# Two attentions over 2048 tokens: a third PSUM bank for the maxima, the causal mask as a matrix product, and the softmax shift as rows of the operands

## What is computed

```python
x = L0_attn_x;  xn = layernorm(x)
# first attention: 16 heads of 8, causal
q, k, v = xn @ Wq.T, xn @ Wk.T * 8**-0.5, xn @ Wv.T
attn = softmax(where(causal, q k^T, -inf))
s = layernorm(attn v) * gamma + beta, then @ Wo.T
# the FFN block: 16 query heads, 4 shared key/value heads, then experts
h = rmsnorm(xn);  q, k, v = h @ Wq + bq, h @ Wk + bk, h @ Wv + bv
q, k = rmsnorm(rope(q)) * qn_w, rmsnorm(rope(k)) * kn_w
out = softmax(where(causal, q k^T / sqrt(8), -inf)) v, gated by sigmoid(out @ Wg + bg)
x1 = xn + out @ Wo + bo
y = the top expert of 8 for each token of rmsnorm(x1)
result = x + s * silu(x1 + y)
```

## Time and profile before

| | us |
|---|---|
| median of 3 runs | 800.93 (800.92 to 801.12) |
| the profiled execution | 802.43 |
| its span, first to last instruction | 800.7 |
| PE (matmuls) busy | 673.8 (84%) |
| VectorE busy | 548.2 (68%) |
| ScalarE busy | 600.1 (75%) |
| GpSimd busy | 184.6 (23%) |
| mean granted clock of TensorE | 0.977 of full |

### The profile page before, as it was taken

The page is one execution under the profiler, slowest core; times in us unless marked ns, Lnnn a source line. Parts: engine busy times, 40 slices in busy tenths (PEclk is TensorE's granted clock), DMA queues, the critical chain, the costliest instruction groups (busy, mean ns, idle before and its releaser), DMA issues.

```text
span 800.7 us, 28924 instructions
## 1 busy us (share of the span) xinstructions
PE 673.8 (84%) x12295; PEld 218.3 (27%) x12295; DVE 548.2 (68%) x1492; ACT 600.1 (75%) x682; POOL 184.6 (23%) x357
## 2 busy tenths in 40 slices
PE   1368877889989899899988888888888988999994
PEld 1122222222222222222222222223232222355542
DVE  6885431777778777676678877777787877545436
ACT  1167977778877788888987787877777687888882
POOL 4363104011012011201120103120032055225241
PEclk9997989999999999999999999999999999999996
DMA  3112224104112000100021001100000050435523
GB/s 117 56 50 61 59 73 150 52 3 78 47 38 63 23 3 6 49 22 2 3 64 33 3 2 48 49 3 2 3 3 2 2 167 27 122 100 172 159 79 89
DMA packets 35852, 41.72 MB, mean 52 GB/s; under 512 B 5916, under 2 KB 26396, under 8 KB 35724
## 3 DMA queue, kind: packets, MB, share of 16 engines
q1 hardware_dynamic: 34052, 36.69, 15.6%
q0 software_dynamic: 1248, 2.57, 1.0%
q10 hardware_dynamic: 424, 0.62, 0.2%
HBM read 29.39 MB, written 10.24 MB: 49 GB/s over the span
## 4 chain that ended last, share of the span: by engine, by line
PE 55%; DVE 19%; ACT 8%; issue 8%; SPq 7%; DMA 2%; POOL 0%; POOLq 0%; ACTq 0%; DVEq 0%
PE PS L1030 25%; PE PS L979 13%; PE PS L1008 8%; ACT PR L908 7%; DVE MP L1349 7%; PE PS L934 6%; DVE PS L1346 4%; SPq L529 2%; SPq L530 2%; PE PS L1040 1%; DMA k_shared<-WORKQ 1%; SPq L532 1%; SPq L533 1%; DVE MP L1346 1%; DVE OT L1370 1%
## 5 line engine op out<-in xcount | busy, mean ns | idle before, releaser
L908 ACT ACTIVATE PR<-PS,QKM 128x1024 f32<-128x1024 f32 (+1 forms) x288 | 287.8, 1068 | 40.3 <-PE PS L1008 39.3
L908 ACT ACTIVATE PR<-PS 128x1024 f32<-128x1024 f32 (+1 forms) x288 | 264.9, 976 | 61.6 <-PE PS L1008 59.5
L1349 DVE TENSOR_REDUCE MP<-PS 128x1 f32<-128x512 f32 x384 | 248.6, 685 | 75.9 <-PE PS L979 73.6
L1030 PE MATMUL PS<-PR,VA 128*18 128x512 f32 (+3 forms) x2560 | 295.0, 543 | 1.2 <-DVE OT L1370 0.6
L1008 PE MATMUL PS<-QA,KA 56*32 56x512 bf16 (+7 forms) x5120 | 237.6, 355 | 31.4 <-ACT PR L908 26.8
L979 PE MATMUL PS<-KA,QA 56*32 56x512 f16 (+3 forms) x2560 | 203.9, 350 | 45.6 <-DVE MP L1349 26.5
L720 POOL TENSOR_SCALAR_AFFINE_SELECT PR<-PR 128x256 f32<-128x256 f32 x256 | 102.3, 417 | 454.7 <-ACT PR L908 452.1
L1346 DVE CUSTOM_DVE_ANT_0 PS<-PS,CON 128x128 f32<-128x128 f32 (+3 forms) x256 | 122.9, 506 | 49.7 <-PE PS L979 46.2
L979 PEld LDWEIGHTS PS<-KA,QA 56*32 56x32 bf16 x2560 | 58.2, 89 | 212.6 <-DVE MP L1349 116.4
L1008 PEld LDWEIGHTS PS<-QA,KA 56*32 56x32 f16 (+1 forms) x5120 | 67.3, 90 | 161.5 <-ACT PR L908 138.5
L1030 PEld LDWEIGHTS PS<-PR,VA 128*18 128x18 f32 x2560 | 46.8, 97 | 94.1 <-issue 87.4
(11 more groups left out here) (178 smaller groups left out, 390.3 us busy)
## 6 DMA issues: line engine op xcount, KB each, us to landing
WORKQ<-in_W SPq DMA_DIRECT2D x16, 450.0 KB, 3.9
QA<-q_parts SPq DMA_DIRECT2D x124, 48.0 KB
WORKK<-in_W SPq DMA_DIRECT2D x7, 450.0 KB, 3.3
KA<-k_parts SPq DMA_DIRECT2D x64, 48.0 KB
q_parts<-WORKQ SPq DMA_DIRECT2D x4, 384.0 KB, 2.9
q_parts<-WORKK SPq DMA_DIRECT2D x4, 384.0 KB, 3.9
expert_tokens<-ZERO SPq DMA_DIRECT2D x1, 1483.5 KB, 10.2
KA<-k_shared SPq DMA_DIRECT2D x60, 24.0 KB
```

The costliest lines, as they stand in the source:

```text
L908: act.activation(PR[:, (2 * n + p) % RING, :, 0:w], PS[:, 2 * p:2 * p + 2, 0:w], ACT.Exp, bias=shift)\
L1030: last = pe.matmul(PS[STRIP * hh:STRIP * hh + 2 * VW, 6, q0:CH], VA[:, slot % 2, kb, hh, VW * (1 - place):VW * (3 - place)], PR[:, (2 * n ...
L1349: dve.reduce_max(top, bank, AX).then_inc(s_mr, 1)
```

## The change

1. `bank_uses` gives each unit the bank of 4, 5 and 7 that was used the longest time ago, by whatever work.
2. Diagonal units get their mask on PE: four more matmuls of 32 rows and 128 columns add a table of 0 and -1e30 to the last 128 columns. The table and a 32 x 32 identity are bf16, loaded by one DMA, and cast by GpSimd at step 22. VectorE uses the plain maximum for all units, and the table of constants is shorter by what the mask took.
3. The FFN's constant shift is written into rows 56 and 57 of `QA` as two bf16 numbers, by four DMAs a buffer: buffers 0 and 1 at the start, buffer 2 when slot 5 is loaded. The FFN's scores use 58 rows, and the exponentials have no bias tile. In buffer 0 the rows still hold the constant when slot 3 comes.
4. The six DMAs of ones go to the start of SP's queue, with eight of the shift behind them.

The diff, cut to its core:

```diff
@@ bank_uses
+    def oldest():
+        return min((4, 5, 7), key=lambda bank: max(i for i, use in enumerate(out) if use[1] == bank))
...
         for u in (*parts[0], *parts[1]):
-            out.append((("unit", unit_number(u)), 4 + unit_number(u) % 2, "M"))
+            out.append((("unit", unit_number(u)), oldest(), "M"))
...
         for u in parts[2]:
-            out.append((("unit", unit_number(u)), 4 + unit_number(u) % 2, "M"))
+            out.append((("unit", unit_number(u)), oldest(), "M"))
@@ sync
             sp.dma_start(LAT[:, :], late).then_inc(s_lc, 16)
+            sp.dma_start(EXTRA[:, 0:NMASK], masks).then_inc(s_ml, 16)
...
+            def constant_shift(b):
+                for row in (STACK, STACK + 1, 64 + STACK, 64 + STACK + 1):
+                    sp.dma_start(QA[row:row + 1, b, :, :, :].rearrange("p c h (t s) -> p (c h t) s", s=P),
+                                 SHB[:, row % 2, :].unsqueeze(1).broadcast_to([1, NC * PAIRS * BPC, P])).then_inc(s_cs, 16)
+
+            sp.wait_ge(s_1b, 1)
+            for b in range(NBUF):
+                ones(b)
+            sp.wait_ge(s_cb2, 1)
+            constant_shift(0)
+            constant_shift(1)
...
-            sp.wait_ge(s_1b, 1)
-            for b in range(NBUF):
-                ones(b)
             for c in range(NC):
                 store_first(c, 0)
...
                         load(sp, k, c, (0, 1))
+                    if k == FFN_SLOT:
+                        constant_shift(k % NBUF)
@@ gpsimd
+                if n == 22:
+                    gp.wait_ge(s_ml, 16)
+                    gp.tensor_copy(MASK[:, :], EXTRA[:, 0:NMASK]).then_inc(s_cm, 1)
@@ scalar
-                        shift = QKM[:, 0:1] if SLOT_GROUP[SEQ[n][0]] < NKV else 0.0
-                        act.activation(PR[:, (2 * n + p) % RING, :, 0:w], PS[:, 2 * p:2 * p + 2, 0:w], ACT.Exp, bias=shift)\
+                        act.activation(PR[:, (2 * n + p) % RING, :, 0:w], PS[:, 2 * p:2 * p + 2, 0:w], ACT.Exp)\
@@ tensor, max_unit
-                bank = PS[:, 4 + u % 2, :]
+                bank = PS[:, BANK["unit", u], :]
...
                     last = pe.matmul(bank[r:r + STRIP, 0:w], QA[rows, b, c, pr, q:q + STRIP],
-                                     KA[rows, b, kc, pr, 0:w], start=True, stop=True)
+                                     KA[rows, b, kc, pr, 0:w], start=True, stop=kc < c)
+                if kc == c:
+                    pe.wait_ge(s_cm, 1)
+                    for r in range(0, P, STRIP):
+                        last = pe.matmul(bank[r:r + STRIP, w - P:w], MASK[64 * e:64 * e + 64, M_EYE:M_EYE + STRIP],
+                                         MASK[64 * e:64 * e + 64, r // STRIP * P:(r // STRIP + 1) * P], start=False, stop=True)
@@ tensor, scores
-                    rows = slice(64 * e, 64 * e + (STACK if ffn else ROWS))
+                    rows = slice(64 * e, 64 * e + ROWS)
@@ vector
+            link(dve.tensor_copy(SHB[:, 0, :], QKM[0:1, 0:1].broadcast_to([1, P])))
+            dve.tensor_tensor(SHB[:, 1, :], QKM[0:1, 0:1].broadcast_to([1, P]), SHB[:, 0, :], ALU.subtract)\
+               .then_inc(s_cb2, 1)
@@ vector, max_unit
-                bank = PS[:, 4 + u % 2, 0:w]
-                if kc == qb // BPC:
-
-                    dve.tensor_tensor_reduce(out=bank, in0=bank, in1=CON[:, K_CM + CH - w:K_CM + CH], scale=1.0, scalar=NEG,
-                                             op0=ALU.add, op1=ALU.max, accum_out=top).then_inc(s_mr, 1)
-                else:
-                    dve.reduce_max(top, bank, AX).then_inc(s_mr, 1)
+                dve.reduce_max(top, PS[:, BANK["unit", u], 0:w], AX).then_inc(s_mr, 1)
```

More of the change, by code:

```diff
@@ L291, with build @@
 NL = 912
-K_ID, K_TRI, K_CM, K_EARLIER, K_BEFORE, K_RANK, K_TOK, K_SPARE, K_TILE, K_J = 0, 128, 256, 768, 904, 968, 976, 992, 1015, 1038
-NK = 1054
-def build(nc, x, front, late, const, W12, out):
+K_ID, K_TRI, K_EARLIER, K_BEFORE, K_RANK, K_TOK, K_SPARE, K_TILE, K_J = 0, 128, 256, 392, 456, 464, 480, 503, 526
+NK = 542
+M_EYE = BPC * P
+NMASK = M_EYE + STRIP
+def build(nc, x, front, late, const, masks, W12, out):
     with ExitStack() as ctx:
@@ L324, in build @@
         ZERO = sb("ZERO", [P, ROW])
+        MASK = sb("MASK", [P, NMASK], BF16)
         ONEB = sb("ONEB", [2, P], F16)
@@ L332, in build @@
         HS = sb("HS", [P, 3, BPC * 20])
+        SHB = sb("SHB", [1, 2, P], BF16)
         SC = sb("SC", [P, 5])
@@ L447, in build @@
         s_one = sem("shift_ones_placed")
+        s_cb2 = sem("constant_shift_built")
+        s_cs = sem("constant_shift_placed")
+        s_ml = sem("masks_loaded")
+        s_cm = sem("masks_cast")
         s_sq2 = sem("key_weights_squared")
@@ L998, in scores @@
                     loaded(slot, c)
-                    if not ffn:
-                        pe.wait_ge(s_one, 32 * NBUF)
+                    pe.wait_ge(s_one, 32 * NBUF)
+                    if ffn:
+                        pe.wait_ge(s_cs, 64 * (2 if slot < FFN_SLOT else 3))
+                    else:
                         before = sum(1 for j in range(slot) if j % NBUF == b and SLOT_GROUP[j] >= NKV)
@@ L1658, in pack_const @@
     a[:, K_TRI:K_TRI + P] = p[None, :] > p[:, None]
-    a[:, K_CM + CH - P:K_CM + CH] = np.where(p[None, :] > p[:, None], NEG, 0.0)
     for t in range(1, T + 1):
@@ L1670, in pack_const, with pack_masks @@
     return a
+def pack_masks():
+    a = np.zeros((2, 64, NMASK), np.float32)
+    i = np.arange(STRIP)
+    for r in range(BPC):
+        a[:, :STRIP, r * P:(r + 1) * P] = np.where(np.arange(P)[None, :] > r * STRIP + i[:, None], NEG, 0.0)
+    a[:, :STRIP, M_EYE:] = np.eye(STRIP)
+    return a.reshape(P, NMASK)
 def kernel(**inputs):
@@ L1679 @@
     named = [("x", i["L0_attn_x"]), ("front", pack_front(i)), ("late", pack_late(i)), ("const", pack_const()),
+             ("masks", pack_masks()),
              ("W12", np.concatenate([i["L0_ffn_W1"],
```

## The result

| | before | changed |
|---|---|---|
| median, us | 800.92 (799.74 to 801.12, 4 runs) | **764.49** (762.16 to 765.30, 4 runs) |
| ratio to before | 1 | 0.9543, 95% interval 0.952 to 0.9567 |
| profiled execution's span, us | 800.7 | 763.1 |

The account below looks back on a forecast made before the run. Time was taken to be lost in handovers, chiefly PE waiting for VectorE to read maxima banks, with no engine full. Terms -28 + 11 - 2 - 10 - 3 + 4 = -28 us took the 800.9 us median to 773, range 752 to 793.

Parts of the forecast that it names:

- first step: In the maxima stretch, 141.9 to 691.0 us, PE, VectorE and ScalarE all have slack; PE waits 42.7 us for VectorE.
- third bank: Maxima units: PE's 42.7 us of waits for VectorE to read a bank fall by two thirds, -28 us (-43 to -10).
- bank 7 not free: Turns, T and FFN works wait for a unit's reduction; ten works at 1.1 us each, +4 us (0 to +11).
- mask on TensorE, with VectorE's side: 256 diagonal units: mask products cost PE +11 us (0 to +14.3); VectorE's plain maxima save -2 us (-10 to 0).
- shift in stack rows: FFN exponentials without a bias tile take 1.023 us instead of 1.116: -10 us (-23.8 to -5.6).
- ones off SP's queue: Before the maxima: six DMAs of ones leave SP's chain at 105.34 us for the start, -3 us (-4.35 to 0).
- the 15 that the text gave as a sign of being right: Sign: PE's waits for maxima fall from 42.7 us to 15 or less.
- The weights in the open: Rival: the mask product's weight load is not hidden, so the mask costs 37 us instead of 11; 799 us, chance 0.05.
- a serialised mask product: Rival: PE finishes the unit before adding the mask, 0.215 us per group, 55 us instead of 11; 817 us, chance 0.06.
- The next wait: Rival: PE arrives earlier and waits for ScalarE's exponentials, so the extra bank gives only 10 us; 798 us, chance 0.09.
- Two more signs: PE's waits for ScalarE grow from 10.8 to 15 to 25 us; the mask line costs PE 15 to 25 us busy alone.

Follow-up runs that it names:

- the first experiment: Only the bank rule changed on the kernel before: units take the least recently used of banks 4, 5 and 7; 776.04 us, ratio 0.9699.

## Why the prediction was right, and where its sizes were off

Its first step, that time is lost in handing over banks and not on an engine, is shown: the third bank alone gives 25 us, and 31 to 33 where it harms nobody. The third bank and the mask turned out better than was taken, bank 7 worse and the rest near; the miss of 8.5 us in the total (764.5 where 773 was forecast) stayed within the range. By terms, each measured on the kernel named, so that they need not add up:

| term | predicted | measured |
|---|---|---|
| third bank | -28 | -31 to -33 (kept off bank 7 where it is wanted, on the kernel before) |
| bank 7 not free | +4 | +7 in the changed kernel, +8 on the kernel before |
| mask on TensorE, with VectorE's side | +11 - 2 | +0.5 alone; +2 to +4 with three banks, not clear of the noise |
| shift in stack rows | -10 | -7 alone, -6 to -12 with three banks |
| ones off SP's queue | -3 | -2.5 |
| sum | -28 | -36.4 as a whole |

*The mask is the term that failed.* The step was: 256 x 0.056 us = 14.3, of which some "runs beside the other half's work", taken at +11, with only -2 for VectorE. Measured, the two together cost 0.5 us. Both sides of it were off.

On TensorE more was covered than I took. In the changed kernel the matmuls of the mask start 0.22 us behind those of their unit, which is 512 columns. Units alternate between the two halves of the rows, and the next one starts beside the product:

```profile
599.67 0.39 PE L1005 MATMUL PS<-KA,QA 56*32 56x512 f16 x4
...
599.89 0.23 PE L1010 MATMUL PS<-MASK 64*32 64x128 bf16 x4
...
599.90 0.39 PE L1005 MATMUL PS<-KA,QA 56*32 56x512 f16 x4
```

From unit to unit that is 0.23 us with a product in between, and it was 0.24 without. Only where the values follow does it show: 0.37 us behind the unit (596.52 to 596.89) where it was 0.33 before. In the kernel with only the mask PE was busy for 7.9 us more between steps 34 and 257 (494.1 against 486.2), 0.031 us a product and not 0.056; and the doubled mask puts the price of a product at 0.016 to 0.03 us of time.

On VectorE the prediction read the earlier trace rows wrongly. It added the 0.141 us of the accumulator's read to the 0.711 of the masked form, and got 43 us. The timeline of the kernel before shows that they overlap, and that the next instruction starts together with the read:

```profile
251.51 0.57 DVE L1346 CUSTOM_DVE_ANT_0 PS<-PS,CON 128x384 f32<-128x384 f32 x1 [0.57 <-PE PS L979]
252.00 0.14 DVE L1346 DVE_READ_ACCUMULATOR2_ANT MP<- 128x1 f32 x1
252.00 0.60 DVE L1346 CUSTOM_DVE_ANT_0 PS<-PS,CON 128x384 f32<-128x384 f32 x1
```

With 512 columns the read starts 0.62 us behind the start of its form (median of 64), and plain maxima that follow one another start 0.61 apart. So a masked form held VectorE hardly longer than a plain one, and its bank came free 0.07 us later (0.76 us after its start against 0.685), not 0.167. The mask product takes nearly all of that back: where VectorE is idle it starts 0.45 us behind a unit's first matmul and 0.50 behind that of a unit with a mask product. From the start of a masked unit to its bank being free it was 0.45 + 0.76 = 1.21 us, and is 0.50 + 0.69 = 1.19. I take this to be why, in a kernel with two banks that waits for this handover, the move was worth nothing. VectorE's busy time in the stretch fell from 417.7 to 402.2 us, 15.6.

*The third bank* took 40 of the 42.7 us that units waited, where two thirds were expected. The bursts of four to seven units, which should have held it back, hardly do: the waits of units are 2.9 us. VectorE's reductions run under the value products, and I take it that three banks hold what PE makes in between. But 15.3 us of waits for a reduction came to other work, so that PE's waits for maxima are 18.2 us in all, more than the 15 that the text gave as a sign of being right; only the units' own pass it.

*Bank 7.* Ten works were counted, at 1.1 us at most each, and 4 us were taken because the other engines go on. They do, but PE's queue holds the scores for ScalarE: ScalarE is idle for 1.91 us at the end of step 232. The upper part of the bound would have been the better value. It also had no term for the clock, which was at 1.2 GHz for 3.4 us of the changed kernel's maxima and for 10 of the first experiment's, both times after such idle time.

*The front.* Of its 3 us for SP 2.5 were there. The rest of the 8.1 us that the two profiles show I put down to the slow front of the profiled execution before (1.5 to 3.5 us) and to what the exponentials without a bias save ahead of step 34; the two were not separated. SP's queue, as forecast, issues 14 small DMAs in the 22 us in which it used to wait, and ends 9 us before the first store; ScalarE's copy that had waited 2.23 us for a late store starts without a wait:

```profile
4.58 5.70 SPq L561 DMA_DIRECT2D KA<-ONEB  x6
11.64 5.05 SPq L566 DMA_DIRECT2D QA<-SHB  x8
25.79 0.40 SPq L578 DMA_DIRECT2D q_parts<-WORKQ  x1
...
120.47 0.69 ACT L844 ACTIVATE WORKK<-PS,SC 128x512 bf16<-128x512 f32 x1
```

*The rivals.* The weights in the open and a serialised mask product are refuted by the timeline above and the doubled mask: the weights of the mask product load at 597.89, while the unit's matmuls on the same row half run from 597.88. So the rule of the Trainium skill ("TensorE: Matmul & The Clock Gate", Part 3, The mechanism), by which weight loads overlap matmuls in flight only when the row group differs, is not borne out here: load and matmul of one row half overlap. The same section also lets a load go ahead that targets a background weight buffer, which would fit; no row tells where these loads went. The next wait did not take over: PE waits 8.3 us for ScalarE in the stretch, less than the 10.8 of the earlier trace rows. Two more signs that the text asked to see did not come: it expected 15 to 25 us there, and 15 to 25 us of PE busy with the mask where it stands alone, which were 7.9.

## What to carry to other kernels

Where three engines are each between three quarters and nine tenths busy, look at the waits between them by line: a third buffer took 40 of the 43 us that its own users waited, and the time fell by 25 us though no engine had less to do. Before a buffer is shared, list who else needs it and what stands behind them on their queue; a rule that looks at the step's other work kept the gain and saved the 7 to 8 us that had been given back. An operation moved from one part-filled engine to another can be worth nothing at all: read its price from where the next instruction starts, not from the sum of durations, and measure it by moving it alone and by doing it twice.

## What the runs showed that was not expected

- Of the nine steps with six or seven units, six are shorter with the third bank, by 0.2 to 0.5 us (204, with seven, took 4.15 us before and 3.97 now). Three are longer, 86, 209 and 220, by 1.0, 1.2 and 0.7, and all three are back within 0.12 us of before where units are kept off bank 7. No kernel with a fourth bank was run.
- The FFN's full steps stand at the length of two exponentials where nothing else holds them: many took 1.99 to 2.01 us before and 1.81 to 1.83 after, 0.09 us less for each of the two, which overlap a little (1.02 us each). Steps of the first attention stood at 1.81 to 1.83 in both.
- A single profiled execution can have a front 3.5 us slower than another with the same program there (step 34 at 141.9 us against 138.4), and that one was 1.5 us above its kernel's median. Small terms were therefore read from medians of several runs.
- TensorE's clock fell to 1.2 GHz between steps 34 and 257 in seven of the thirteen profiled executions (an eighth, with only the ones moved, was at 1.2 GHz from 134.1 to 140.9 us, across step 34). It did so for 3.4 us in the changed kernel (532.9), in the one with the mask doubled (536.7) and in the one with the bias tile of zeros (173.2); for 10 in the one with only the bank rule; for 6.8 in the one with the rule that looks at the other work, on the kernel before; for 3.4 twice in the one with only the shift (478.2 and 607.9); and for 3.4, 6.8 and 3.4 in the changed kernel with the mask on VectorE (171.7, 530.1, 564.3). In the kernel before, the one with only the mask and the three changed ones with units kept off bank 7 it stood at 2.4 GHz throughout. So two banks do not prevent it, and the kernel with the bias tile had the same wait of 1.38 us (until 539.53) without it. What settles which execution has such a stretch stays open. Where it falls into steps 206 to 240, their times are not the price of waits alone.
